# Layer 1's three experts of a token from the eight-largest and replace-first-occurrence instructions of VectorE

## What is computed

```python
def _L1_ffn_ref(x, router_W, router_b, ...):          # 15 experts, K = 3
    logits = xt @ router_W + router_b                 # [4096, 15]
    probs = jax.nn.softmax(logits / T, axis=-1)
    top_p, top_i = jax.lax.top_k(probs, K)
    cw = jnp.zeros((n, E)).at[jnp.arange(n)[:, None], top_i].set(top_p)
    ...                                               # all experts are run, weighted by cw
    routed = jnp.einsum('ned,ne->nd', ye, cw)
    return (shared + routed).reshape(b, l, d)
```

## Time and profile before

| what | value |
|---|---|
| three runs, median (lowest to highest) | 1788.06 us (1779.5 to 1792.17) |
| the profiled execution | 1786.1 us, of it 1783.9 us from the first to the last instruction |
| busy share PE, DVE, ACT, POOL | 85%, 64%, 49%, 25% |
| chain that ended last, by engine | PE 61%, DVE 16%, issue 8%, POOL 5%, ACT 4%, DMA 3% |
| granted clock of TensorE, mean | 0.924 of full speed |

### The profile page before, as it was taken

One profiled execution on the slowest core, in us unless ns is written; L12 is line 12 of the kernel. 1 busy time (PEld: TensorE's weight loads), 2 busy tenths in 40 slices (PEclk: granted clock), 3 DMA queues, 4 the chain that ended last, 5 costly groups with the idle time before them and its releaser, 6 DMA issues.

```text
span 1783.9 us, 41485 instructions
## 1 busy us (share of the span) xinstructions
PE 1510.5 (85%) x11849; PEld 960.7 (54%) x11849; DVE 1149.9 (64%) x3192; ACT 866.0 (49%) x1971; POOL 444.5 (25%) x542
## 2 busy tenths in 40 slices
PE   5456999999989749999995779999899699999998
PEld 4123666665655247888885245555554255555554
DVE  6734666765767865565565556566667577777774
ACT  1023444443444314444441145555555268888887
POOL 3475322322322202222222622121222110000000
PEclk9998999998989659999995589999999789999998
DMA  8442454553544003332320333333442011111110
GB/s 255 132 156 72 146 172 124 156 160 121 158 146 134 2 17 133 137 142 101 136 95 21 97 99 117 103 112 124 130 130 76 21 51 49 50 52 48 48 52 10
DMA packets 127956, 182.17 MB, mean 102 GB/s; under 512 B 14825, under 2 KB 107297, under 8 KB 125425
## 3 DMA queue, kind: packets, MB, share of 16 engines
q1 hardware_dynamic: 94944, 141.94, 24.6%
q10 hardware_dynamic: 26112, 25.17, 4.9%
q0 software_dynamic: 6816, 14.02, 2.2%
HBM read 145.84 MB, written 42.84 MB: 106 GB/s over the span
## 4 chain that ended last, share of the span: by engine, by line
PE 61%; DVE 16%; issue 8%; POOL 5%; ACT 4%; DMA 3%; DVEq 1%; SPq 0%; ACTq 0%; POOLq 0%
PE pH L529 7%; PE pO L738 7%; PE pH L621 7%; PE pY L542 6%; PE pT_ L595 6%; PE pY L629 6%; POOL sorted_x L994 4%; DVE mx L1330 3%; PE pS L703 3%; PE pS L681 3%; ACT pex L852 2%; PE pT_ L593 2%; PE pT_ L513 2%; DVE ob L1408 1%; PE pY L550 1%
## 5 line engine op out<-in xcount | busy, mean ns | idle before, releaser
L852 ACT ACTIVATE pex<-pT_ 128x512 f32<-128x512 f32 (+1 forms) x768 | 427.1, 560 | 476.7 <-PE pT_ L595 363.5
L1330 DVE TENSOR_REDUCE mx<-pS 128x2 f32<-128x512 f32 x512 | 346.8, 688 | 139.2 <-PE pS L572 122.8
L595 PE MATMUL pT_<-stk 32*128 32x256 f16 x1024 | 199.1, 283 | 72.0 <-DMA stk<-packed_qk 29.4
L893 POOL DMA_INDIRECT home_y<-ysb,home x117 | 115.1, 984 | 545.5 <-DVE ysb L1352 345.7
L572 PE MATMUL pS<-stk 32*128 32x256 f16 x1024 | 207.2, 289 | 22.5 <-DVEq L1073 17.5
L738 PE MATMUL pO<-pex,va 128*9 128x256 f32 (+1 forms) x3072 | 202.2, 384 | 2.7 <-ACT pex L852 2.7
L845 ACT ACTIVATE wb<-pH,b 128x256 f32<-128x256 f32 x256 | 107.3, 470 | 113.5 <-PE pH L529 113.1
L595 PEld LDWEIGHTS pT_<-stk 32*128 32x128 f16 x1024 | 55.1, 93 | 184.6 <-issue 87.1
L529 PE MATMUL pH<-XT,w 128*128 (+1 forms) x512 | 132.3, 386 | 1.0
L621 PE MATMUL pH<-xsT,wb 128*128 128x128 f32 x888 | 132.1, 294 | 0.3 <-ACT xsT L821 0.3
L629 PE MATMUL pY<-wb,hbs 128*128 128x128 f32 x888 | 128.6, 288 | 3.0 <-DVE ysb L1352 3.0
(11 more groups left out here) (216 smaller groups left out, 2630.0 us busy)
## 6 DMA issues: line engine op xcount, KB each, us to landing
wb<-in_w SPq DMA_DIRECT2D x111, 514.0 KB, 4.8
stk<-packed_qk ACTq DMA_DIRECT2D x96, 256.0 KB, 2.7
packed_qk<-qk SPq DMA_DIRECT2D x144, 128.0 KB, 2.0
wb<-gates_turned SPq DMA_DIRECT2D x8, 2048.0 KB, 7.0
pex<-gates_turned SPq DMA_DIRECT2D x8, 2048.0 KB, 7.0
xsb<-sorted_x SPq DMA_DIRECT2D x111, 64.5 KB, 2.1
sorted_x<-in_c_places SPq DMA_DIRECT2D x4, 1548.0 KB, 16.5
XN<-home_y SPq DMA_DIRECT2D x16, 256.0 KB, 5.2
```

The source lines that it names most:

```text
L595: return pe.matmul(bank[:, part * T:(part + 1) * T], key, stk[rows, side, j, 0:T], start=True, stop=True)
L852: ins = act.activation(pex[:, k % 8, 0:n], bank[:, 0:n], ACT.Exp)
L893: pool.indirect_dma_start(YH, bass.IndirectOffsetOnAxis(ap=home[:, place_:place_ + 1], axis=0), ysb[:, place_, :], None).then_inc(sem(f"ho ...
L1330: ins = dve.tensor_reduce(mx[:, :, j, col], bank.rearrange("p (c n) -> p c n", c=2), AX.X, ALU.max)
```

## The change

In layer 1 alone, after the probabilities are there, the loop of three rounds is left and the following runs instead. `pr` and `ra` are widened from 16 to 24 elements a tile. Five elements behind a tile's 15 probabilities are set to -1. For each of the 16 tiles of the half `dve.max` writes the eight largest of the 15 probabilities, in falling order, into `highest` (part of `rb`), counted and not waited for one by one. After one wait the places 3 to 7 of each eight are overwritten by -1. Then for each tile `dve.match_replace` copies 20 elements of `pr` to `ra` with the first occurrence of each of the eight values replaced by -2: the three largest, and five of the fillers. After one more wait `GA` is set to the probability where `ra` is negative, and to zero elsewhere.

```diff
-        pr = sb("pr", [P, NT, 16])
+        pr = sb("pr", [P, NT, 24])
...
-        ra, rb, rc = (sb(n, [P, NT, 16]) for n in ("ra", "rb", "rc"))
+        ra = sb("ra", [P, NT, 24])
+        rb, rc = (sb(n, [P, NT, 16]) for n in ("rb", "rc"))
...
                 chain.link(dve.tensor_tensor(p_, p_, full_e(r2), ALU.mult))
+                if l == 1:
+                    tiles, highest, wide = range(NT)[half], rb[:, :, 0:8], n + 8 - TOPK[l]
+                    chain.link(dve.memset(pr[:, half, n:wide], -1.0))
+                    for t in tiles:
+                        m = chain.mark(dve.max(highest[:, t, :], pr[:, t, 0:n]))
+                    chain.wait(m)
+                    chain.link(dve.memset(highest[:, half, TOPK[l]:8], -1.0))
+                    for t in tiles:
+                        m = chain.mark(dve.match_replace(ra[:, t, 0:wide], highest[:, t, :], pr[:, t, 0:wide], -2.0))
+                    chain.wait(m)
+                    chain.link(dve.scalar_tensor_tensor(g_, a_, 0.0, p_, ALU.is_lt, ALU.mult))
+                    return
                 for k in range(TOPK[l]):
```

## The result

Over 20 runs of each kernel the median went from 1792.15 us (1778.47 to 1802.39) to 1782.59 us (1771.49 to 1795.34); the ratio is 0.9962, 95% interval 0.9944 to 0.9981, 6.8 us less with an interval of 3.4 to 10.0. (The ratio is not the quotient of the two medians: these differ by 9.6 us, and the means of the same runs by 8.1 us. Single runs of either kernel scatter with a standard deviation of 5.8 us, so one comparison does not settle 2 us.) The prediction had 1776.3 from 1786.1, a ratio of 0.9945: it lies at the edge of that interval, and by the ratio about two thirds of the forecast 9.8 us arrived. The profiled execution has a span of 1781.4 us, 2.5 us less than the one of before.

A forecast was written before the change was run, and what follows sets the result against it. TensorE bounds most of the kernel, but VectorE's choice bounds the layer 0 to 1 gap. Each half falls from 9.71 to 4.80 us, 9.8 us together: 1786.1 - 9.8 = 1776.3, given as 1777 us, range 1767 to 1789.

The forecast's parts named there:

- What bounds, and where the gain is taken: Layer 0 to 1 passage: PE and POOL idle during VectorE's two loops, so time saved there shortens the kernel.
- The price of the new instructions: Layer 1's choice: a half costs 4.80 us in place of 9.71, a gain of 9.8 us for both.
- 32 x 0.119 = 3.81 us: Each half's 16 eight-largest and 16 replacements, one instruction each, priced at the scan's 0.119 us from start to start.
- Rival 1: Each replacement fills two places in VectorE's list: a half costs 6.70 us, together 6.0 us gained, 1780.1 us; chance 0.35.
- Rival 2: The choice's new instructions don't overlap or are long: 0.7 to 1.3 us slower, 1786.8 to 1787.4 us; chance 0.10.
- Rival 3: TensorE's clock comes back sooner after the shorter gap, adding 3 us to the 9.8: 1773.3 us; chance 0.08.
- Rival 4: Gain lost behind the signal, for instance in the gates' 6.65 us spread: 1786.1 us; chance 0.05.
- so the gain should come out at the end whole: Behind the choice: everything moves forward as a block, turns last as before, so all 9.8 us reach the end.
- so I charge no wait for code: VectorE's list: 26 more instructions, 0.12 us apart, costed at no wait for instruction fetches.
- The number: Whole kernel: 1777 us, the middle of 1776.3 (from the profiled execution) and 1778.3 (from the median of three runs).

The follow-up runs named there:

- no choice: Changed kernel with layer 1's choice left out, all 15 experts weighted by one instruction a half (another output); ratio 0.9869 to the kernel before.
- threshold kernel: Changed kernel without fillers, second memset and replacements; a gate is the probability where at least the third largest; ratios 0.9906 and 0.9935 to the kernel before.

## Why the prediction was right or wrong

**What bounds, and where the gain is taken: right.** PE and POOL stood still through both halves, and the stretch from the first tile to POOL's first copy shortened by the choice's own saving in every variant, from 5.0 us (one half) to 18.5 us (none). Layer 1's turns were 279.5 us after 279.7 before. The four comparisons of the changed kernel, weighted by the inverse square of their intervals' half-widths, give 0.9963 with a half-width of 0.0010, 6.6 us of 1791; 10.0 us less in the choice and 3.4 us more in layer 3 make the same 6.6. The match to a tenth is chance, with 1.8 and some 2 us of scatter on the two sides; but the four together exclude 10.0 us.

**The price of the new instructions: the sum right, by two errors that cancel.** A half was put at 4.80 us and took 4.70. The term "32 x 0.119 = 3.81 us" had the interval too long and the number too small. Sixteen eight-largest take 1.30 us together, each 0.158 us long, so (1.30 - 0.158) / 15 = 0.076 us from start to start; a load and a pass together 0.148 to 0.149 us from tile to tile (0.159 us for the first load). That is 16 x (0.076 + 0.149) = 3.60 us for 48 instructions at 0.075 us in the mean. The scan, taken as the nearest row for its carried state, was the wrong neighbour: the earlier trace rows has the aggregate at 0.09 us, and that was nearly the price of one instruction. From the Trainium skill's section on the errata in "VectorE: DVE Perf Modes", 58 cycles plus the elements, the estimate is 73 cycles or 0.076 us for the first, and 66 + 78 cycles or 0.150 us for the pair: the trace agrees with both within 2 ns. The prediction had applied it to one instruction per replacement.

**Rival 1, two places in the list: true as a mechanism, wrong as a price.** The trace has 32 loads and 32 passes. The Trainium skill, in "VectorE: DVE Perf Modes", the section on two Vector instructions with no wait between them, says that the load and the pass are two instructions; the trace agrees. At the scan's interval this would have left 6.0 us; at the true one the choice gains 10.0.

**Rival 2, no overlap: false**, and measured. With a wait behind each one the two halves cost 7.9 us more, which would have left 2.1 us of the gain.

**Rival 3, an earlier clock in layer 1: false.** The turns were as long with a gap of 14 us (278.4 to 280.3 us) as with one of 24 (278.3 to 280.1), and not shorter with 5.4 us (281.5 us with no choice). The clock does move them, by some 3 us, but not by the gap's length alone: they take 278.3 to 278.7 us in the four profiles in which it did not fall a second time (one with a gap of 14 us, three with 24), and 281.5 us in the two in which it stayed at 0.50 twice as long as in the rest when it fell (gaps of 5.4 and 19 us). **Rival 4, the gates' spread: not borne out**, 6.65 us and then 6.71; over all profiles it takes 6.6 to 7.3 us.

**What failed** is the last step, "so the gain should come out at the end whole", and in it the sentence "so I charge no wait for code", a term put at nothing. It had asked only whether VectorE itself would be short of code behind the shorter instructions, and nothing in the choice shows that it was. But the place of a fetch moves with the count of instructions, and in the changed kernel one falls on a write that PE waits for, some 770 us behind the change. In its place the runs show layer 3 longer by 3.4 us in the mean: 0.8 us for PE's wait, which moved with the code, and most of the rest for a clock that comes back some 10 us later in five of seven profiles with the wait, and in two of eleven without, and costs 3.4 us each time. That the wait brings the late clock about is what the profiles suggest; it stays open. No case had a loss outside the changed stretch and the signal's followers. With the code 66 instructions longer the same change had a ratio of 0.9942, the forecast being 0.9945; but the interval, 0.9917 to 0.9967, also holds the 0.9963 of the unmoved kernel.

**The number** also started too low. The middle between the profiled execution and the median of three runs was taken as the base; over 20 runs the kernel before had 1792.15 us, 4 us above that median. That the change would stay within 1% came true, by 0.4%; what the prediction did not weigh is that enough runs tell 0.4% from nothing.

**A better version.** The threshold kernel beats both: ratios 0.9906 and 0.9935, together 0.9922 with a half-width of 0.0018, some 14 us under the kernel before. It keeps only the eight-largest, and its fetch happens to fall clear of the write. Its layer 2 took 463.9 and 464.1 us where the other kernels on the same two chips took 459.9 to 462.9; that was not followed. It differs from the change in one case: two experts with exactly the third largest probability would both be taken.

## What to carry to other kernels

When a dependent chain of whole-width instructions computes a small selection, special instructions per tile can be cheaper even sixteen times over, as long as none waits for the one before: here the 48 instructions of a half cost 3.6 us, and 60 more waits in the two halves cost 7.9 us. Count what a call expands to, and price it by the cheapest small row in a run without waits, not by the one that looks most alike. And treat a gain or loss of a few microseconds at the end as unproven until the stages are measured one by one, in more than one profile: here changing the number of instructions moved later code fetches, so test with padding that does nothing before crediting or blaming the edit.

## What the runs showed of the hardware that was not expected

- Where a fetch of instructions of one packet (0.01 MB) fell on a write of 3 x 128 KB, the write's end was drawn out by 0.6 to 0.9 us (at 4 to 16 GB/s in the two shown), and the read behind it was issued 3.4 to 3.7 us after the write in place of 2.84, in seven profiles of seven. The fetch fell 31.8 to 32.3 us behind layer 3's first tile in all seven, on different chips.
- With a wait on the instruction directly ahead, one MAX8 starts 0.211 us after the last in place of 0.076 us, and a load and replacement 0.275 us in place of 0.148; MAX8 lasts 0.177 us behind a wait and 0.156 to 0.158 us in a row.
- TensorE's clock, down at the start of layer 3, was back before 48 us in eleven profiles and not in seven, for the same work; the late return (49 to 50 us in place of 39 to 41, once 46) cost 3.4 us within layer 3's first 60 us, and whether it came went with the moment of the clock's first fall as well as with PE's wait; without the collision layer 3 took 386.2 and 387.4 us in the two late ones and 383.2 to 386.5 in the others.
